# Message stage of a four-layer graph kernel: VectorE copies the turned outer products out of PSUM, and 45 instead of 40 columns of a chunk are summed on TensorE

## The chip, the cores and the metric

The kernel runs on one core of a Trainium2 chip. The metric is the device time in microseconds (us) of one execution. The median of three runs before the change is 27402.7 us. One further execution was profiled; all rows shown here come from it.

## The reference, cut to what matters

Four graph layers are applied in turn to 12500 nodes with 16 features; 400000 edges (`src`, `dst`), sorted by `dst`, are the same in all. Every layer is added to its input. Two of them matter here.

Layer 1 (a sheaf layer) computes two 16-vectors per edge from the features of its two ends and sums one over `src`, one over `dst`. Layer 2 computes a message per edge and sums it over `src`:

```
x_j = h[dst]                                         # 400000 x 16
m   = einsum('ei,ej,ijh->eh', x_j, edge_attr, W)     # outer product 16 x 8 = 128, times W (128 x 16)
m   = silu(m * norm)
agg = segment_sum(m, src)                            # 12500 x 16; W_msg_lin is applied after the sum
u   = silu(einsum('ni,nh,ihk->nk', h, agg, W_upd) * norm2) @ W_upd_lin
x   = x + h + u
```

## The kernel before

**Tiling.** Edges lie on 128 partitions with 3125 columns each (`EP`); a column is one edge per partition. A chunk is `CH` = 125 columns, so both layers run over `NCH` = 25 chunks. All engines have a program of their own over the chunks; the first three chunks are written out, the others are a hardware loop with two chunks in a turn (`chunks`, ring 2). Engines meet at semaphores only, and every engine works strictly in the order of its program.

**The message stage** is `message_edges` (L1711 and on). A chunk is cut into `GR` = 32 groups of 4 columns (the last has 1). For group q:

- VectorE multiplies features and edge attributes to the outer product `PM` (L1909, tile `outer`),
- TensorE transposes it, one 128x128 per column, into PSUM (L1780, `outerT_ps`),
- ScalarE copies that to SBUF (L1848, `outerT`),
- TensorE multiplies by `W_message` (L1790, `message_ps`; `second` in the code),
- ScalarE applies silu and writes `edge_values` (L1830).

`outer`, `outerT_ps` and `outerT` have two buffers each, `message_ps` and `sums_ps` have one.

**Two ways to sum over `src`.** A chunk's first `EQC` = `CH - MT2` = 85 columns are summed within the column first: in groups of `ACCS` = 5, VectorE compares the column's 128 sources with each other (`equal`, L1065, `equal_src`), TensorE multiplies this by the values (`sums`, L1799, `sums_ps`), ScalarE copies the result to `column_sums` (`sums_out`, L1837), and GpSimd adds each column to memory by an indirect DMA (`scatter_pool`, L1199, one DMA a column). The group g is due at step `need[g] + 2`, which gives steps 3 to 23 for the 17 groups.

The other `MT2` = 40 columns are "tiles". For a tile ScalarE makes a one-hot of 1568 node rows in two instructions (L1127 Abs, L1129 Relu; `onehot_act`, a ring of 5 buffers `placed_row`); VectorE splits the values in three bf16 parts and spreads them on 8 lanes (`lane_values`, L1118, per 5 tiles); TensorE adds three parts times four column blocks, 12 matmuls (`tile_sum`, L1141), into PSUM, where the sum stays until the stage ends. The tiles of chunk k are worked off during chunk k+1, spread over its groups by `tiles[q] = range(q * MT2 // GR, (q + 1) * MT2 // GR)`. After chunk 24 its own tiles follow in a tail, then `keep_sums`, `turn_sums` and `store_sums`.

**Order by engine in a step s** (0 to 32) of a chunk:

- TensorE (`products`): `transposes(s)`, `second(s-1)`, the `sums` that are due, then `tile_sum` for `tiles[s-1]` of the chunk before.
- ScalarE (`step`): copy of group s, `silu(s-1)`, the `sums_out` due, then `onehot_act` for `tiles[s]`.
- VectorE (`compute`), ahead of all groups: copy of source and row indices (L1881, L1884; the latter waits until GpSimd has begun the chunk before, `s_chunk`), 16 scans of the features (L1886), then, after the last silu of the chunk before, the split of the tile values (L1890, L1892, L1106, L1108) and the bits of the tile's sources (L1091 to L1096, L1902). Then for each q: `outer` (waits for the transposes of group q-2), the `equal` with `need[g] == q`, the `lane_values` due.
- GpSimd: 85 scatters a chunk, each round of 5 after its `column_sums`.
- SyncE: loads of starts and attributes, and of `src_rows` for `equal`.

**Layer 1** uses the same helpers with its own count of tiles, `MT` = 50, which does not change. It takes `EQC` too: `o.sums = EQC // ACCS` (L1022) is the number of `equal`/`sums` groups at the end of each of its chunks. It scatters 75 columns; groups 15 and 16 (columns 75 to 84) serve only to find, for layer 2, which rows of a column are the first of their source (`CNT`, L1518, L1625 to L1631).

Of the kernel before, what the change touches and what calls it, by code (L numbers as in the profile page):

```python
# [23 lines left out]
ACT = mybir.ActivationFunctionType  # L24
# [3 lines left out]
P = 128  # L28
# [6 lines left out]
CH = 125  # L35
# [4 lines left out]
BIG = 1e30  # L40
HID = 256
ACCS = 5
MT2 = 40
MT = 50
PARTS = 3
Q8 = NP // 8
EQC = CH - MT2
assert EP * P == E and NCH * CH == EP and EQC % ACCS == 0 and MT >= MT2 and (CH - MT) % ACCS == 0


def bcast(ap, shape):
    return ap.to_broadcast(shape)
# [32 lines left out]
def first(k, n):  # L85

    return isinstance(k, int) and k < n


class Kernel:  # L90
# [5 lines left out]
    def sb(self, name, shape, dt=F32, ctx=None):  # L96
        self.uid += 1
        return (ctx or self.ctx).enter_context(self.nc.sbuf_tensor(f"{name}_{self.uid}", shape, dt))
# [5 lines left out]
    def sem(self, name, ctx):  # L104
        self.uid += 1
        s = ctx.enter_context(self.nc.semaphore(f"{name}_{self.uid}"))
        if s.num in self.sem_seen:
            self.sem_old.append(s)
        self.sem_seen.add(s.num)
        return s  # L110
# [1600 lines left out]
    def message_edges(self, Wm, NE_):  # L1711
        nc = self.nc
        W = D + 1
        norm = (D * NE_) ** -0.5
        with ExitStack() as c:
# [5 lines left out]
            PT = [sb(f"outerT{b}", [P, 512]) for b in range(2)]  # L1721
# [5 lines left out]
            o.SRC = srcc  # L1727
            self.tile_buffers(c, o, MT2, [sb(f"placed_row{i}", [P, Q8], BF16)[:] for i in range(5)])
            o.LN = [sb(f"src_row_negative{b}", [P, MT2]) for b in range(2)]
            o.s_abs, o.s_lo = sem("distances_ready"), sem("src_rows_split")  # L1730
            VT, s_vt = sb("matmul_values", [P, MT2, D]), sem("tile_values_ready")
            parts = sb("value_parts", [P, PARTS, MT2, D], BF16)
            keep, turn = sb("node_sums", [P, Q8]), sb("node_rows", [P, -(-Q8 // P) * P])
            tp = [self.ps(f"outerT_ps{i}", [P, 512], c) for i in range(2)]
# [3 lines left out]
            s_used, s_v, s_pm, s_t, s_pt, s_m, s_ms = (sem(x) for x in (  # L1738
                "inputs_used", "dve_chain", "outer_ready", "transposed", "transposed_copied", "message_ready", "message_copied"))
            s_d0 = self.dsem("first_dst_in")  # L1740
            GR, GS = -(-CH // 4), o.sums
# [4 lines left out]
            with self.block() as block:  # L1746
# [74 lines left out]
                @block.scalar  # L1821
                def _(a):
                    def silu(k, q):
                        n = min(4, CH - 4 * q)
                        if q == 0 and not first(k, 1):
                            a.wait_ge(o.s_sum, k * GS)
                        a.wait_ge(s_m, k * GR + (q + 1))
                        if 4 * q + n > SC and not first(k, 1):
                            a.wait_ge(s_vt, k * 2 - 1)
                        nc.scalar.activation(VAL[:, 4 * q:4 * q + n, :], mp[:, 0:n * D].rearrange("p (a b) -> p a b", b=D),  # L1830
                                             ACT.Silu, scale=norm).then_inc(s_ms, 1)

                    def sums_out(k, b, g):
                        if g == 0 and not first(k, 2):
                            a.wait_ge(o.s_chunk, k - 1)
                        a.wait_ge(o.s_sum, k * GS + (g + 1))
                        nc.scalar.activation(o.SV[b][:, ACCS * g:ACCS * (g + 1), :], sm_ps[:, 0:ACCS * D].rearrange("p (a b) -> p a b", b=D),  # L1837
                                             ACT.Copy).then_inc(o.s_sv, 1)

                    def step(k, b):  # L1840
                        for s in range(GR + 1):
                            if s < GR:
                                n = min(4, CH - 4 * s)
                                r = (b + s) % 2
                                a.wait_ge(s_t, k * GR + (s + 1))
                                if not first(k, 1) or s >= 2:
                                    a.wait_ge(s_m, k * GR + (s - 1))
                                nc.scalar.activation(PT[r][:, 0:n * P], tp[r][:, 0:n * P], ACT.Copy).then_inc(s_pt, 1)  # L1848
                            if s >= 1:
                                silu(k, s - 1)  # L1850
                            for g in range(GS):
                                if need[g] + 2 == s:
                                    sums_out(k, b, g)
                            if s < GR and not first(k, 1):
                                if s == 0:
                                    a.wait_ge(o.s_lo, k * 1)
                                for i in tiles[s]:
                                    self.onehot_act(a, o, k - 1, 1 - b, i)
                    chunks(a, NCH, 3, step)
                    a.wait_ge(o.s_lo, NCH)  # L1860
                    for i in range(MT2):
                        self.onehot_act(a, o, NCH - 1, (NCH - 1) % 2, i)

                @block.vector
                def _(v):
# [5 lines left out]
                    def compute(k, b):  # L1871
# [29 lines left out]
                        self.src_bits(v, w, o, srcc[:, SC:CH], b)  # L1901
                        w(v.tensor_scalar(o.LN[b][:], o.LO[b][:], -1.0, None, ALU.mult))  # L1902
                        v.sem_inc(o.s_lo, 1)
                        for q in range(GR):
                            n = min(4, CH - 4 * q)
                            r = (b + q) % 2
                            if not first(k, 1) or q >= 2:
                                v.wait_ge(s_t, k * GR + (q - 1))
                            v.tensor_tensor(PM[r][:, 0:n], bcast(XF[b][:, 4 * q:4 * q + n, :].unsqueeze(3), [P, n, D, NE_]),  # L1909
                                            bcast(EA[b][:, 4 * q:4 * q + n, :].unsqueeze(2), [P, n, D, NE_]), ALU.mult).then_inc(s_pm, 1)  # L1910
                            for g in range(GS):
                                if need[g] == q:
                                    self.equal(v, o, k, b, g)
                            if not first(k, 1):
                                for i in tiles[q]:
                                    if i % ACCS == 0:
                                        self.lane_values(v, o, k - 1, 1 - b, i // ACCS, parts)
                        v.wait_ge(s_pm, k * GR + GR)
                        v.sem_inc(s_used, 1)
                        if first(k, 1):  # L1920
                            K[0] = w.n
                        assert w.n == K[0]
                    chunks(v, NCH, 3, compute)
                    k, b = NCH - 1, (NCH - 1) % 2
                    v.wait_ge(s_ms, NCH * GR)
# [403 lines left out]
```

## Time and profile before

| | us |
|---|---|
| median of 3 runs | 27402.7 |
| range of the 3 runs | 27401.45 to 27413.41 |
| profiled execution, its own time | 27386.06 |
| span of its trace | 27384.3 |
| start of the first and of the last scatter (layer 1; message stage) | 9942.0; 22361.6 |
| message stage, first outer product to release of the next block | 18217.0 to 22368.4 |

Over the whole span GpSimd is busy 73%, TensorE 39%, VectorE 33%, ScalarE 31%. These are averages over stages with different limits; the message stage alone looks quite different, as its window below shows. In the profile, PE is TensorE's matmul, PEld its weight load (each matmul of these small shapes has one, and consecutive loads show the pace of TensorE), DVE VectorE, ACT ScalarE, POOL GpSimd. A timeline row is: start, duration, engine, line, operation, tiles, count, and in brackets the idle time ahead of it and what ended it. ScalarE and VectorE start an instruction a little before the one ahead has ended, so the pace is read from start to start.

### The profile page before, as it was taken

What the parts mean: (1) busy time and instruction counts of PE and PEld (TensorE: products, weight loads), DVE (VectorE), ACT (ScalarE), POOL (GpSimd) and SP (SyncE); (2) the same over time, 40 slices, a digit from 0 to 9 for tenths busy, and PEclk for the clock granted to TensorE, in tenths of its full rate; (3) what the DMA queues carried; (4) which work ended last, traced back from release to release, by engine and by line L of the source; (5) the groups of instructions that cost most, each with busy time, mean ns of one, the idle gap of its engine ahead of it and who ended that gap; (6) DMA issues with size and microseconds to landing.
All of it is one profiled execution on the core that took longest, in us unless ns stands there. A gap on an engine that the chain in (4) does not pass through costs nothing. (4 is left out here: it accounts for less than half of the span.)

```text
span 27384.3 us, 206288 instructions
## 1 busy us (share of the span) xinstructions
PE 10673.4 (39%) x61414; PEld 7318.9 (27%) x61414; DVE 9052.7 (33%) x15004; ACT 8400.1 (31%) x8986; POOL 20052.3 (73%) x17824
## 2 busy tenths in 40 slices
PE   0000000100000057777776676749998874000004
PEld 0000000100000034444444444436666653000003
DVE  2333333222222133333333333324433322333331
ACT  0000000000000035555555555638888860000001
POOL 5777776677777577777777777568888863777775
PEclk9999999555555568888888778869999987555557
DMA  2111111111111112222222222123333324666664
GB/s 79 30 30 36 30 30 31 18 27 27 27 30 27 22 29 29 29 29 29 29 29 29 32 36 30 22 49 49 51 50 50 49 24 131 204 207 203 203 207 123
DMA packets 2038400, 1639.07 MB, mean 60 GB/s; under 512 B 868362, under 2 KB 1838548, under 8 KB 2020260
## 3 DMA queue, kind: packets, MB, share of 16 engines
q0 software_dynamic: 1061008, 588.28, 15.9%
q10 hardware_dynamic: 818050, 577.62, 6.4%
q1 hardware_dynamic: 158354, 460.98, 4.9%
q8 instruction: 499, 8.18, 0.1%
q14 instruction: 489, 4.01, 0.0%
HBM read 938.69 MB, written 686.90 MB: 59 GB/s over the span
## 5 line engine op out<-in xcount | busy, mean ns | idle before, releaser
L1199 POOL DMA_INDIRECT acc<-column_sums,sum_rows x4000 | 6639.9, 1660 | 1441.3 <-issue 1179.9
L717 POOL DMA_INDIRECT gathered<-gat_table,src_index x6250 | 6052.3, 968 | 2053.5 <-issue 2053.5
L1141 PE MATMUL node_sums<-placed_row,lane_values 128*128 128x392 bf16 x27000 | 5155.9, 345 | 1193.0 <-ACT placed_row L1129 1079.8
L1419 POOL DMA_INDIRECT gathered<-sheaf_table,src_index x3125 | 3156.4, 1010 | 1233.5 <-issue 875.7
L2137 POOL DMA_INDIRECT gathered<-message_table,src_index x3125 | 3062.1, 980 | 984.7 <-issue 951.7
L1127 ACT ACTIVATE placed_row<-iota_rows,src_row_negative 128x1568 bf16<-128x1568 f32 x2250 | 3582.3, 1592 | 269.7 <-PE node_sums L1141 205.4
L1141 PEld LDWEIGHTS node_sums<-placed_row,lane_values 128*128 128x128 bf16 x27000 | 2620.1, 103 | 3477.1 <-ACT placed_row L1129 1558.0
L1129 ACT ACTIVATE placed_row<-placed_row 128x1568 bf16<-128x1568 bf16 x2250 | 3397.5, 1510 | 71.1
L829 PE MATMUL histogram<-high_onehot,low_onehot 128*128 128x98 bf16 x3125 | 368.4, 279 | 7793.2 <-DVE high_onehot L743 7793.2
L816 ACT ACTIVATE decays<-decays 128x375 f32<-128x375 f32 (+1 forms) x50 | 20.6, 412 | 8226.1 <-DVE weights L787 8226.1
L829 PEld LDWEIGHTS histogram<-high_onehot,low_onehot 128*128 128x128 bf16 x3125 | 235.1, 131 | 7926.3 <-DVE high_onehot L743 7926.3
L777 DVE TENSOR_TENSOR scores<-alpha_dst,gathered 128x375 f32<-128x375 f32 (+1 forms) x50 | 34.8, 696 | 5633.9 <-DMA gathered<-gat_table,src_index 5633.9
L567 PE MATMUL transposed<-ident,last_rows 128*128 128x128 f32 (+3 forms) x5 | 2.2, 442 | 4223.6 <-DVE sums L599 4223.6
L2154 DVE SCALAR_TENSOR_TENSOR gathered<-gathered,same 128x256 f32<-128x256 f32 x3000 | 1472.1, 491 | 107.2
L1475 PE MATMUL hidden_row_ps<-vectors,equal_src 128*128 128x19 f32 x4250 | 911.3, 380 | 1157.8 <-DVE equal_src L1065 1065.2
L2270 ACT ACTIVATE sumsT<-ps 128x512 f32<-128x512 f32 x49 | 29.3, 597 | 4084.0 <-PE ps L2238 4084.0
L1909 DVE TENSOR_TENSOR outer<-dst_features,edge_attr 128x512 f32<-128x512 f32 (+1 forms) x800 | 543.4, 679 | 2175.3 <-PE outerT_ps L1780 2169.8
L1475 PEld LDWEIGHTS hidden_row_ps<-vectors,equal_src 128*128 128x128 f32 x4250 | 908.5, 333 | 1178.4 <-DVE equal_src L1065 1037.2
L1118 DVE TENSOR_TENSOR lane_values<-lane_onehot,products 128x640 bf16<-128x640 bf16 x750 | 572.2, 821 | 1898.0 <-PE node_sums L1141 1892.0
L567 PEld LDWEIGHTS transposed<-ident,last_rows 128*128 128x128 f32 (+3 forms) x5 | 0.7, 149 | 4225.2 <-DVE sums L599 4225.2
L1579 DVE COPY vectors<-vectors_ps 128x512 f32<-128x512 f32 x200 | 138.4, 692 | 2628.1 <-PE vectors_ps L1458 2628.1
L1455 PEld LDWEIGHTS vectors_ps<-W_blocks,hidden 128*128 128x128 f32 x6400 | 822.9, 194 | 364.8 <-issue 199.1
(397 smaller groups left out, 17322.3 us busy)
## 6 DMA issues: line engine op xcount, KB each, us to landing
message_rows<-gathered ACTq DMA_DIRECT2D x250, 1600.0 KB
src_rows<-src_rows SPq DMA_DIRECT2D x225, 640.0 KB
src_rows<-src_rows SPq DMA_DIRECT2D x125, 960.0 KB
gathered<-gat_table,src_index POOLq DMA_INDIRECT x6250
gat_rows<-scanned ACTq DMA_DIRECT2D x25, 3375.0 KB
acc<-column_sums,sum_rows POOLq DMA_INDIRECT x4000, 3.1
gat_rows<-scanned ACTq DMA_DIRECT2D x25, 2125.0 KB, 6.8
start_values<-starts SPq DMA_DIRECT2D x50, 1062.5 KB, 5.0
```

The costliest lines, as they stand in the source:

```text
L717: g.indirect_dma_start(G[b][:, j, :], None, tab, bass.IndirectOffsetOnAxis(ap=IX[b][:, j:j + 1], axis=0)).then_inc(s_g[b], 16)
L829: last = pe.matmul(hp[:, 0:NT], OL[ob][:, j, :], OH[ob][:, j, :], start=opening and j == 0, stop=False, skip_group_check=True)
L1118: ins = v.tensor_tensor(o.SVH[r][:, i], bcast(o.E8[:, a:a + ACCS, :].unsqueeze(3), [P, ACCS, 8, D]), bcast(parts[:, i, a:a + ACCS, :].unsq ...
L1127: self.nc.scalar.activation(o.OW[r], o.IO[:], ACT.Abs, bias=o.LN[b][:, i:i + 1]).then_inc(o.s_abs, 1)
L1129: self.nc.scalar.activation(o.OW[r], o.OW[r], ACT.Relu, scale=-1.0, bias=1.0).then_inc(o.s_mv, 1)
L1141: last = pe.matmul(o.acc[:, m, 0:Q8 // 4], lane, o.OW[r][:, m * (Q8 // 4):(m + 1) * (Q8 // 4)], start=first(k, 1) and i == 0 and part == 0 ...
L1199: g.indirect_dma_start(self.acc[i], bass.IndirectOffsetOnAxis(ap=o.IXS[b][:, j:j + 1], axis=0), o.SV[b][:, j, :], None, compute_op=ALU.add ...
L1419: g.indirect_dma_start(G[b][:, j, :], None, self.tab17, bass.IndirectOffsetOnAxis(ap=IX[b][:, j:j + 1], axis=0)).then_inc(s_g[b], 16)
L1455: last = pe.matmul(vp[:, (4 * i + j) * 32:(4 * i + j + 1) * 32], R[j % 2][:, i * P:(i + 1) * P], W2b[:], start=i == 0 and j == 0, stop=Fal ...
L1475: last = pe.matmul(pre[g % 2][:, j * DW:(j + 1) * DW], o.EQ[g % o.nq][:, j, :], VAL[:, g * ACCS + j, :], start=True, stop=True)
L2137: g.indirect_dma_start(G[b][:, j, :], None, self.qtab, bass.IndirectOffsetOnAxis(ap=IX[b][:, j:j + 1], axis=0)).then_inc(s_g[b], 16)
L2154: v.scalar_tensor_tensor(G[b][:, j, :], before, SM[b][:, j:j + 1], G[b][:, j, :], ALU.mult, ALU.add).then_inc(s_v, 1)
```

## The change

Two things. ScalarE's program loses the copy of `outerT_ps`; VectorE's gets it as `turned(q)`, with the same two waits (for the transposes of q, and for the product that read the buffer two groups ago). In VectorE's order `turned(q - 1)` stands behind `outer` of group q and ahead of `equal` and `lane_values` of q; `turned(31)` stands behind the loop, ahead of the next chunk's work. And `MT2` is 45, so that `EQC` is 80: 16 groups of sums (due at steps 3 to 21) and 80 scatters a chunk in the message stage, 45 tiles, 9 `lane_values`; and 16 groups in each chunk of layer 1.

```diff
-MT2 = 40
+MT2 = 45
@@ ScalarE, step
                         for s in range(GR + 1):
-                            if s < GR:
-                                n = min(4, CH - 4 * s)
-                                r = (b + s) % 2
-                                a.wait_ge(s_t, k * GR + (s + 1))
-                                if not first(k, 1) or s >= 2:
-                                    a.wait_ge(s_m, k * GR + (s - 1))
-                                nc.scalar.activation(PT[r][:, 0:n * P], tp[r][:, 0:n * P], ACT.Copy).then_inc(s_pt, 1)
                             if s >= 1:
                                 silu(k, s - 1)
@@ VectorE, compute
                         v.sem_inc(o.s_lo, 1)
+                        def turned(q):
+                            n = min(4, CH - 4 * q)
+                            r = (b + q) % 2
+                            v.wait_ge(s_t, k * GR + (q + 1))
+                            if not first(k, 1) or q >= 2:
+                                v.wait_ge(s_m, k * GR + (q - 1))
+                            v.tensor_copy(PT[r][:, 0:n * P], tp[r][:, 0:n * P]).then_inc(s_pt, 1)
                         for q in range(GR):
...
                                             bcast(EA[b][:, 4 * q:4 * q + n, :].unsqueeze(2), [P, n, D, NE_]), ALU.mult).then_inc(s_pm, 1)
+                            if q:
+                                turned(q - 1)
                             for g in range(GS):
...
+                        turned(GR - 1)
                         v.wait_ge(s_pm, k * GR + GR)
                         v.sem_inc(s_used, 1)
```

## Rows read from the trace of the kernel before

**Rows 1.** Windows, message stage: us; busy PE, PEld, DVE, ACT, POOL; clock, DMA, GB/s.

```profile
18640.00:20880.00 2240.00, 2038.49 (x14374) 1526.52 (x14372) 889.73 (x1466) 2003.80 (x2259) 1889.42 (x1151) 0.96 0.34 51
```

**Rows 2.** Groups by line in 19000 to 21000: busy, mean ns, idle before and releasers.

```profile
L1199 POOL DMA_INDIRECT acc<-column_sums,sum_rows x1027 | 1687.6, 1643 | 313.1 <-issue 298.1 <-DMA acc<-column_sums,sum_rows 11.6 <-ACT column_sums L1837 3.4
```

**Rows 3.** Timeline of DVE: last outer products of chunks 1, 16, 24; two copies.

```profile
18477.22 0.29 DVE L1909 TENSOR_TENSOR outer<-dst_features,edge_attr 128x128 f32<-128x128 f32 x1 [5.97 <-PE outerT_ps L1780]
...
20874.20 0.29 DVE L1909 TENSOR_TENSOR outer<-dst_features,edge_attr 128x128 f32<-128x128 f32 x1 [5.97 <-PE outerT_ps L1780]
20877.73 0.23 DVE L1881 COPY src_chunk<-srcf 128x125 f32 x1 [3.24 <-issue]
...
22041.29 0.23 DVE L1884 COPY sum_rows<-sidx 128x125 int32 x1 [14.00 <-POOLq L1198]
...
22191.67 0.29 DVE L1909 TENSOR_TENSOR outer<-dst_features,edge_attr 128x128 f32<-128x128 f32 x1 [5.97 <-PE outerT_ps L1780]
```

**Rows 4.** Timeline of one step with sums and one tile, ACT and PEld.

```profile
20004.34 1.59 ACT L1127 ACTIVATE placed_row<-iota_rows,src_row_negative 128x1568 bf16<-128x1568 f32 x1
...
20005.84 0.53 PEld L1780 LDWEIGHTS outerT_ps<-ident,outer 128*128 128x128 f32 x4
...
20007.22 1.20 PEld L1799 LDWEIGHTS sums_ps<-edge_values,equal_src 128*128 128x128 f32 x10
...
20007.38 0.58 ACT L1848 ACTIVATE outerT<-outerT_ps 128x512 f32<-128x512 f32 x1
20007.86 0.21 ACT L1830 ACTIVATE edge_values<-message_ps 128x64 f32<-128x64 f32 x1
...
20008.26 1.86 PEld L1141 LDWEIGHTS node_sums<-placed_row,lane_values 128*128 128x128 bf16 x12
...
20008.56 0.24 ACT L1837 ACTIVATE column_sums<-sums_ps 128x80 f32<-128x80 f32 x1 [0.48 <-PE sums_ps L1799]
...
20010.19 0.52 PEld L1780 LDWEIGHTS outerT_ps<-ident,outer 128*128 128x128 f32 x4
```

**Rows 5.** Timeline: second tile of a step, from its Relu to its matmuls.

```profile
20017.71 1.51 ACT L1129 ACTIVATE placed_row<-placed_row 128x1568 bf16<-128x1568 bf16 x1
...
20019.27 1.77 PEld L1141 LDWEIGHTS node_sums<-placed_row,lane_values 128*128 128x128 bf16 x12 [0.44 <-ACT placed_row L1129]
```

**Rows 6.** Timeline from one chunk to the next, and the next chunk's last silu.

```profile
20077.28 0.29 DVE L1909 TENSOR_TENSOR outer<-dst_features,edge_attr 128x128 f32<-128x128 f32 x1 [5.97 <-PE outerT_ps L1780]
...
20085.39 0.26 ACT L1848 ACTIVATE outerT<-outerT_ps 128x128 f32<-128x128 f32 x1
...
20091.94 0.49 DVE L1890 COPY matmul_values<-edge_values 128x640 f32<-128x640 f32 x1 [7.48 <-ACT edge_values L1830]
...
20098.38 0.69 DVE L1909 TENSOR_TENSOR outer<-dst_features,edge_attr 128x512 f32<-128x512 f32 x1 [0.23 <-DVE src_row_negative L1902]
...
20104.67 0.22 ACT L1830 ACTIVATE edge_values<-message_ps 128x64 f32<-128x64 f32 x1
...
20250.38 0.17 ACT L1830 ACTIVATE edge_values<-message_ps 128x16 f32<-128x16 f32 x1
```

**Rows 7.** Windows: the ten microseconds after a chunk change.

```profile
20100.00:20110.00 10.00, 8.38 (x45) 5.99 (x44) 7.01 (x11) 8.83 (x10) 8.47 (x6) 0.65 0.49 103
```

**Rows 8.** Groups of the page: a copy of this size on DVE.

```profile
L1579 DVE COPY vectors<-vectors_ps 128x512 f32<-128x512 f32 x200 | 138.4, 692 | 2628.1 <-PE vectors_ps L1458 2628.1
```

**Rows 9.** Timeline of the stage's end: second store of tile sums, last scatter, next block.

```profile
22335.70 0.75 SPq L1177 DMA_DIRECT2D acc_matmul<-node_rows  x1
...
22361.64 1.55 POOL L1199 DMA_INDIRECT acc<-column_sums,sum_rows  x1 [0.30 <-issue]
22368.40 11.99 SPq L1220 DMA_DIRECT2D acc_in<-acc  x5
```

**Rows 10.** Timeline of layer 1's groups of sums, one of them.

```profile
12191.94 0.83 DVE L1065 TENSOR_TENSOR equal_src<-src_rows,src_chunk 128x640 f32<-128x640 f32 x1 [1.31 <-PE hidden_row_ps L1475]
```

**Rows 11.** Waits of POOL in 12000 to 14000: us, times, longest.

```profile
POOL gathered L1419 <- DVEq L1632: 70.7, 6, 14.3
```

## The prediction

> **What bounds the kernel now.** The page's shares are averages over stages, so the message stage is read by itself, in five views.
>
> First its window [rows 1]: in 2240 us PE is busy 2038, ACT 2004, POOL 1889, DVE 890. Three engines are nearly full; which of them ends last can't be told from shares. Second, the groups by line [rows 2]: POOL issued 1027 scatters in 2000 us, 1.95 us each, and its idle time is almost all "issue", the gap between two of its own instructions; it waited for ACT 3.4 us in all. So POOL never starves: 85 scatters take 165.5 us. Third, the chunk's length, read at the last outer product [rows 3]: from chunk 1 to 16 it is (20874.20 - 18477.22) / 15 = 159.8 us, from chunk 16 to 24 (22191.67 - 20874.20) / 8 = 164.7 us. TensorE, ScalarE and VectorE (the lattice, below) make a chunk in 159.8, POOL falls 5.7 behind in each, and once it is a chunk behind, VectorE waits for it ahead of its row indices (14.00 us at 22041.29). Fourth, the end [rows 9]: the next block starts 6.8 us after the last scatter; the tile sums were stored some 26 us sooner. So POOL sets the stage, but the lattice is only 5.7 us a chunk shorter.
>
> Fifth, the timeline of one step [rows 4], which gives prices from start to start. TensorE: transposes and products of a group 1.38 (05.84 to 07.22), a group of sums 1.04 (to 08.26), a tile 1.93 (to 10.19). ScalarE: a one-hot 3.04 (04.34 to 07.38), the copy 0.48 (to 07.86), silu and column sums about 0.11 each when not waiting (between 0 and their busy 0.21 and 0.24). In this step both need 4.35: TensorE because 1.38 + 1.04 + 1.93 is that, ScalarE with 0.48 of waiting for the sums. Before the change a chunk has 12 such steps, 11 with one tile and no sums (3.04 + 0.48 + 0.11 = 3.63, ScalarE last) and 8 with two tiles (6.67, ScalarE last): 52.2 + 39.9 + 53.4 = 145.5. The trace has 20250.38 - 20104.67 = 145.7 from the first silu to the last [rows 6]. The prices can be trusted.
>
> **The change, part by part.**
>
> *POOL.* 5 scatters fewer a chunk: 80 x 1.947 = 155.8. Alone this takes the stage down to the lattice's pace, since that now ends last; so all depends on what the lattice becomes.
>
> *ScalarE.* Loses 31.25 x 0.48 = 15.0 and one column sum, gains 5 x 3.04 = 15.2: its work stays as it was, 142 us.
>
> *TensorE.* 5 tiles more, one group of sums less: 5 x 1.93 - 1.04 = +8.6 us a chunk. This is no longer covered: steps 3 to 21 hold 27 tiles and 16 sums, 19 x 1.38 + 16 x 1.04 + 27 x 1.93 = 94.9 us for TensorE against 27 x 3.04 + 19 x 0.11 + 16 x 0.11 = 86 for ScalarE. TensorE ends last in all of them. ScalarE can't run ahead through it: its silu of step s follows TensorE's product in the same step, so a step with two tiles hands over late. From Relu to the matmuls it takes 1.56 [rows 5]; worked through for the 8 steps with two tiles in that stretch (2, 4, 7, 9, 12, 14, 17, 19), the second tile comes 0.2 to 0.3 late each time, 2.3 in all. So 97.2. Ahead of it stand 6.0 from the first silu to step 3 (unchanged). Behind it, steps 22 to 31 have no sums and 15 tiles: ScalarE last, 15 x 3.04 + 9 x 0.11, 1.7 to start, and five times 0.1 to 0.5 in which TensorE is late after a pair, 1.7 together: 50.0. First to last silu: 6.0 + 97.2 + 50.0 = 153.2. The same walk over the old order gives 145.1, so the step costs 8.1. The bounds: if hand-overs are free, TensorE's and ScalarE's stretches give 149.2, +4; if every step costs the later engine's price (2.42 + 3.86 for the two-tile steps with sums, 6.2 for those without), +10.
>
> *Chunk change.* From the last silu VectorE splits the tile values and prepares the bits, 20091.94 to 20098.38, then outer, transposes, copy, product, silu, 20104.67 [rows 6]. Five of the ops in it work on 40 columns and now on 45: a tenth of about 5 us, +0.6; the copy moves to VectorE at 0.69 us (a copy of this size there [rows 8]) against 0.58 and stands behind lane_values and a second outer, +0.1. Between +0.3 and +1.5; I take +0.7.
>
> *The copy on VectorE within a chunk.* 31 x 0.69 + 0.29 = 22 us a chunk beside 64 busy of 160: hidden by idle time. What stands behind each is equal (0.82) and lane_values (2.3); outer of group q+1 is then done at most 5 us after the transposes of q-1, and TensorE wants it 6.6 after. PT is ready 1.6 after the transposes, and its product comes at least 3.3 after. Nothing, if that holds; if not, up to 1 us in each of 9 groups.
>
> *The copy at the end of a chunk.* turned(31) now stands ahead of the next chunk's scans. In [rows 6] VectorE was done with outer 31 at 77.57, and with the scans 7.48 before it was let go by the last silu, at 84.5. It will start them only after the copy of group 31 (ACT made it at 85.39; VectorE can at about 84.2), that is 7 us later. So the cover shrinks from 7.48 to about 0. In each second chunk, at the end of the hardware loop's turn, VectorE has another 3.24 us of issue [rows 3]: this stood in the cover and now is bare, 3.2 / 2 = +1.6 a chunk. Bounds 0 and 3.2.
>
> Together 8.1 + 0.7 + 1.6 = +10.4: a chunk of 170.2, TensorE and ScalarE last, POOL (155.8) well inside. Even if every added copy stretched one scatter from 1.55 to 1.80, POOL would need 164.
>
> *The stage.* 23 chunk distances x 10.4 + 8.8 for the first (its change is short) = +248. The pushback goes: 8 x (164.7 - 159.8) = -39. The first chunk, without tiles, loses one group of sums, -2. The tail: TensorE's and ScalarE's end now decides, not POOL's. Its store was issued at 22335.70; with the same 6.8 to the next block that is 22342.5, plus 5 tiles x 3.04 = 15.2, plus 2.0 because the last silu lies further behind the last outer: 22359.7 against 22368.4, -9. Sum +198.
>
> *Layer 1.* One group of 17 less. The groups pass at 0.83 + 1.31 = 2.14 us [rows 10], VectorE, TensorE and ScalarE in turn, and VectorE goes on from the last to the next chunk. POOL has 70.7 / 6 = 11.8 us of slack a chunk there, waiting for VectorE [rows 11], so it doesn't hold this back. 25 x 2.14 = -54. Bounds 0 and -60 (narrower index work besides).
>
> Net +198 - 54 = +144 on the profiled execution's 27386.1, which lies 16.6 under the median; the same on the median 27402.7 gives 27547, I say 27545.
>
> Of TensorE's clock [rows 7]: after a chunk change 0.65 of full is granted in ten us, so part of it at 1.2 GHz; before, TensorE had sat idle some 5 us. It will idle as long, and 3 us longer in each second chunk. The Trainium skill (TensorE: Matmul & The Clock Gate, Part 1) says that the clock follows how busy the array has been of late. By that rule the slow stretch grows in those chunks; the row agrees that it exists, and can't show the growth.
>
> The Trainium skill (VectorE: DVE Perf Modes, the errata's table) prices a PSUM source at 120 + elements cycles on VectorE and 172 + elements on ScalarE's faster clock: 0.66 against 0.57 us here. The trace agrees (0.69 and 0.58); the rule speaks against the move, and by it the copies cost VectorE 20 us a chunk, still hidden.
>
> **The rivals.**
>
> *TensorE hides the tiles (the faster side).* It is idle 9% of the window [rows 1], 14 us a chunk, more than the added 8.6. If this idle time is usable in the sums' stretch, a chunk stays at 159.8 and the stage loses the pushback: 27402.7 - 39 - 2 - 9 - 54 = 27299. Against it: half of the idle time lies at the chunk change and the rest in steps where ScalarE is last, not in steps 3 to 21. It decides only if a step with sums goes on at 4.35 while it holds 1.42 tiles on average, which is 5.16 by price. If POOL were last even so, at 155.8, it would be 27299 - 24 x 4.0 = 27203.
>
> *Only TensorE's price is paid.* Hand-overs cost nothing, and VectorE's back edge is covered: +4.7 to 6.5 a chunk. With 6: 24 x 6 - 39 - 11 - 54 = +40, 27443. For it: five buffers for one-hots. Against it: ScalarE's order ties it to TensorE's step, and the late second tile is there in [rows 5].
>
> *Dearer chunk change.* Scans bare in every chunk (the copy of 31 waits, +3.2 instead of 1.6), slow clock for one more step (+2): +3.6 x 24 = 86 more, 27630. With layer 1's gain lost as well it would be 27685.
>
> **How the numbers follow.** Forecast 58%, at 27545, its own range 27480 to 27600. TensorE hides 8%, POOL last 2%: faster. Only TensorE's price 17%, of which two thirds within 0.2% (0.2%, 55 us, is about what a measurement of this kernel tells from no change: 27348 to 27458). Dearer change 15%. So faster 0.10, same 0.13, slower 0.77. The range for 8 in 10 is 27430 to 27625: it leaves out the faster side and the far end of the dearer one.
>
> **What would show it.** The last outer products 170 us apart, without idle time at POOL's index wait. PEld without gaps in the steps with sums, and ACT waiting there for message_ps and sums_ps. POOL waiting for column_sums, 14 us a chunk. DVE's wait for the last silu near 0 in place of 7.48. The next block released by the store of tile sums. In layer 1, chunks 2.1 us shorter. It would be wrong if chunks were at 160 or less, if ScalarE had no waits in the sums' stretch, or if VectorE's outer came late in mid-chunk.

## The result and the profile after

| | before | after |
|---|---|---|
| median, us | 27401.4 | 27506.0 |
| range of 6 runs each | 27397.48 to 27413.41 | 27483.06 to 27519.65 |
| span of the profiled execution | 27384.3 | 27484.5 |

The ratio is 1.0037 (95% interval 1.0026 to 1.0047): 104.6 us slower, where +144 was forecast. In the traces the next block is released 107.4 us later, and this divides so: the message stage starts 54.3 sooner (first outer product at 18162.70 in place of 18217.0), the way from there to the last outer product of chunk 0 is 1.4 shorter, the 24 distances from that one to the last outer product of chunk 24 add up to 4041.8 in place of 3866.8 (+175.0), and the tail is 11.9 shorter. -54.3 - 1.4 + 175.0 - 11.9 = +107.4. What follows the release is 7.2 shorter, which gives the +100.2 of the spans. The stage alone, from its first outer product to the release, is 4313.1 in place of 4151.4, +161.7.

The 54.3 are themselves two things. These are the last gather of layer 0 and layer 1's first group of sums, before and then after:

```profile
9132.99 0.95 POOL L717 DMA_INDIRECT gathered<-gat_table,src_index  x1 [0.30 <-issue]
...
9887.90 1.56 DVE L1065 TENSOR_TENSOR equal_src<-src_rows,src_chunk 128x640 f32<-128x640 f32 x2
```

```profile
9146.31 0.94 POOL L717 DMA_INDIRECT gathered<-gat_table,src_index  x1 [0.30 <-issue]
...
9900.59 1.56 DVE L1065 TENSOR_TENSOR equal_src<-src_rows,src_chunk 128x640 f32<-128x640 f32 x2
```

From that group to the first outer product of the message stage it takes 8262.1 in place of 8329.1, so layer 1 is 66.9 shorter. But it starts 12.7 later, and that lateness is there at the end of layer 0 already (13.3), in which the change alters nothing. The same point lay up to 20 us apart in the traces of e5 to e8 (10675.0 to 10695.5), which have the same layer 0 too, so it is scatter between executions.

The first view is the window of the stage, columns as in [rows 1]:

```profile
18600.00:20960.00 2360.00, 2148.80 (x15042) 1578.84 (x15041) 1180.12 (x1946) 2007.24 (x1932) 1841.04 (x1128) 0.97 0.31 46
```

VectorE's share went from 40% to 50%, TensorE's stayed at 91%, ScalarE's fell from 89 to 85% and GpSimd's from 84 to 78%. Who lost its cover stands in the groups by line and in the waits (line waited for: us in total, times, longest), both of 19000 to 21000:

```profile
L1199 POOL DMA_INDIRECT acc<-column_sums,sum_rows x949 | 1548.8, 1632 | 440.3 <-issue 267.1 <-ACT column_sums L1837 157.4 <-DMA acc<-column_sums,sum_rows 15.8
```

```profile
DVE outerT L1903 <- PE outerT_ps L1780: 955.8, 315, 5.5
ACT edge_values L1830 <- PE message_ps L1790: 194.3, 154, 12.4
POOL acc L1199 <- ACT column_sums L1837: 157.4, 21, 16.7
PE outerT_ps L1780 <- DVE outer L1909: 106.6, 24, 9.4
ACT column_sums L1837 <- PE sums_ps L1799: 83.0, 94, 0.9
DVE matmul_values L1883 <- ACT edge_values L1830: 2.0, 6, 0.3
```

GpSimd, which waited for ScalarE 3.4 us in [rows 2], now waits 157.4, that is 13 us a chunk: it no longer sets the pace, and its scatters aren't slower for VectorE's added copies (1632 ns against 1643). ScalarE waits for TensorE's products. TensorE waits for an outer product 24 times in 12 chunks, which is twice at each chunk change and never within a chunk, and the waits show none for one of VectorE's copies. Of VectorE's wait for the last silu (7.48 in [rows 6]) at most 0.3 is left.

The pace, from VectorE's timeline as in [rows 3] (last outer products of chunks 1, 11, 12 and 24):

```profile
18430.47 0.28 DVE L1909 TENSOR_TENSOR outer<-dst_features,edge_attr 128x128 f32<-128x128 f32 x1
...
20116.36 0.28 DVE L1909 TENSOR_TENSOR outer<-dst_features,edge_attr 128x128 f32<-128x128 f32 x1
...
20283.48 0.28 DVE L1909 TENSOR_TENSOR outer<-dst_features,edge_attr 128x128 f32<-128x128 f32 x1
...
22310.96 0.28 DVE L1909 TENSOR_TENSOR outer<-dst_features,edge_attr 128x128 f32<-128x128 f32 x1
```

The mean distance is (22310.96 - 18430.47) / 23 = 168.7; from chunk 4 on 167.1 and about 170.8 take turns, 169.0 on average, and there is no later stretch with a slower pace, as there was with 164.7 before.

One step with sums and two tiles, loads of TensorE and ScalarE's instructions, to be laid beside [rows 4, 5]:

```profile
20046.33 0.53 PEld L1780 LDWEIGHTS outerT_ps<-ident,outer 128*128 128x128 f32 x4
...
20047.71 1.20 PEld L1799 LDWEIGHTS sums_ps<-edge_values,equal_src 128*128 128x128 f32 x10
...
20048.74 1.86 PEld L1141 LDWEIGHTS node_sums<-placed_row,lane_values 128*128 128x128 bf16 x12
20049.48 1.51 ACT L1129 ACTIVATE placed_row<-placed_row 128x1568 bf16<-128x1568 bf16 x1
20050.90 0.21 ACT L1830 ACTIVATE edge_values<-message_ps 128x64 f32<-128x64 f32 x1
20051.00 0.23 ACT L1837 ACTIVATE column_sums<-sums_ps 128x80 f32<-128x80 f32 x1
20051.04 1.77 PEld L1141 LDWEIGHTS node_sums<-placed_row,lane_values 128*128 128x128 bf16 x12 [0.43 <-ACT placed_row L1129]
...
20052.88 0.53 PEld L1780 LDWEIGHTS outerT_ps<-ident,outer 128*128 128x128 f32 x4
```

The prices are those of before: 1.38 to the sums, 1.03 to the first tile. The second tile is late for its Relu. The step takes 6.55 where the prices give 1.38 + 1.04 + 3.86 = 6.28: 0.27 late, within the 0.2 to 0.3 that was forecast.

Two chunk changes, one within the loop's turn and one at its end:

```profile
20125.20 0.29 DVE L1903 COPY outerT<-outerT_ps 128x128 f32<-128x128 f32 x1 [5.52 <-PE outerT_ps L1780]
20125.55 0.23 DVE L1874 COPY src_chunk<-srcf 128x125 f32 x1
...
20132.20 0.17 ACT L1830 ACTIVATE edge_values<-message_ps 128x16 f32<-128x16 f32 x1
...
20132.40 0.54 DVE L1883 COPY matmul_values<-edge_values 128x720 f32<-128x720 f32 x1 [0.33 <-ACT edge_values L1830]
...
20145.39 0.22 ACT L1830 ACTIVATE edge_values<-message_ps 128x64 f32<-128x64 f32 x1 [9.99 <-PE message_ps L1790]
...
20292.32 0.29 DVE L1903 COPY outerT<-outerT_ps 128x128 f32<-128x128 f32 x1 [5.53 <-PE outerT_ps L1780]
20295.69 0.23 DVE L1874 COPY src_chunk<-srcf 128x125 f32 x1 [3.07 <-issue]
...
20299.32 0.17 ACT L1830 ACTIVATE edge_values<-message_ps 128x16 f32<-128x16 f32 x1
...
20302.42 0.54 DVE L1883 COPY matmul_values<-edge_values 128x720 f32<-128x720 f32 x1
...
20315.85 0.22 ACT L1830 ACTIVATE edge_values<-message_ps 128x64 f32<-128x64 f32 x1 [11.84 <-PE message_ps L1790]
```

The first to the last silu, 20145.39 to 20299.32, takes 153.9. The change takes 13.2 in the first case. In the second, after 3.07 of issue, the scans end after the silu that VectorE used to wait for, and the change takes 16.5. The clock granted around the first silu of a chunk (a window that lies to it as that of [rows 7] does, from 4.67 us ahead of it) is 0.57, lower than the 0.65 of [rows 7]:

```profile
20140.72:20150.72 10.00, 8.38 (x40) 5.90 (x39) 6.69 (x11) 3.30 (x4) 4.70 (x3) 0.57 0.14 4
```

The end of the stage, against [rows 9]:

```profile
22339.09 1.55 POOL L1199 DMA_INDIRECT acc<-column_sums,sum_rows  x1 [0.30 <-issue]
...
22470.98 0.66 SPq L1177 DMA_DIRECT2D acc_matmul<-node_rows  x1
22475.80 11.74 SPq L1220 DMA_DIRECT2D acc_in<-acc  x5
```

The last scatter is over 135 us before the next block starts. That starts 4.8 after the store of the tile sums.

### The profile page after: what moved, and what is told of

Same layout as the page of the kernel before. It is cut to its first block and busy times, and to the rows that moved or that the text cites. A ratio compares the mean times of both kernels' runs of the same rounds, so it can differ in the third digit from the quotient of the medians.

```text
span 27484.5 us, 208040 instructions
## 1 busy us (share of the span) xinstructions
PE 10857.1 (40%) x62414; PEld 7393.0 (27%) x62414; DVE 9540.5 (35%) x15829; ACT 8407.1 (31%) x8386; POOL 19794.9 (72%) x17699
## 5 line engine op out<-in xcount | busy, mean ns | idle before, releaser
L1199 POOL DMA_INDIRECT acc<-column_sums,sum_rows x3875 | 6419.4, 1657 | 1684.0 <-issue 1130.8
L1141 PE MATMUL node_sums<-placed_row,lane_values 128*128 128x392 bf16 x28500 | 5421.0, 344 | 1159.9 <-ACT placed_row L1129 1038.9
L1127 ACT ACTIVATE placed_row<-iota_rows,src_row_negative 128x1568 bf16<-128x1568 f32 x2375 | 3777.9, 1591 | 277.0 <-PE node_sums L1141 198.6
L1141 PEld LDWEIGHTS node_sums<-placed_row,lane_values 128*128 128x128 bf16 x28500 | 2772.8, 103 | 3552.7 <-ACT placed_row L1129 1525.3
L1129 ACT ACTIVATE placed_row<-placed_row 128x1568 bf16<-128x1568 bf16 x2375 | 3586.3, 1510 | 75.1
L816 ACT ACTIVATE decays<-decays 128x375 f32<-128x375 f32 (+1 forms) x50 | 20.6, 412 | 8219.1 <-DVE weights L787 8219.1
L2157 DVE SCALAR_TENSOR_TENSOR gathered<-gathered,same 128x256 f32<-128x256 f32 x3000 | 1469.7, 490 | 107.4
L1903 DVE COPY outerT<-outerT_ps 128x512 f32<-128x512 f32 (+1 forms) x800 | 541.9, 677 | 2017.9 <-PE outerT_ps L1780 1998.6
```

Source lines behind the costliest of these rows:

```text
L1127: self.nc.scalar.activation(o.OW[r], o.IO[:], ACT.Abs, bias=o.LN[b][:, i:i + 1]).then_inc(o.s_abs, 1)
L1129: self.nc.scalar.activation(o.OW[r], o.OW[r], ACT.Relu, scale=-1.0, bias=1.0).then_inc(o.s_mv, 1)
L1141: last = pe.matmul(o.acc[:, m, 0:Q8 // 4], lane, o.OW[r][:, m * (Q8 // 4):(m + 1) * (Q8 // 4)], start=first(k, 1) and i == 0 and part == 0 ...
L1199: g.indirect_dma_start(self.acc[i], bass.IndirectOffsetOnAxis(ap=o.IXS[b][:, j:j + 1], axis=0), o.SV[b][:, j, :], None, compute_op=ALU.add ...
L2157: v.scalar_tensor_tensor(G[b][:, j, :], before, SM[b][:, j:j + 1], G[b][:, j, :], ALU.mult, ALU.add).then_inc(s_v, 1)
```

## The experiments

The experiments ran on three chips (e1 to e4, e5 to e8, and e9 and e10), and there everything but the message stage took longer than in the first runs, for the kernel before as for all others: its medians are 29697.5, 29379.8 and 29351.7 in place of 27401.4. In the traces the message stage begins some 1500 to 2000 us later and what follows it is some 380 longer. So totals are compared only with those of before beside them. The message stage is nearly the same everywhere (4313.1, and 4314.9 for the changed kernel run again), and its length, from first outer product to release, is compared directly.

| run | stage, us | chunks, us | ratio of totals (95%) |
|---|---|---|---|
| before | 4151.4 | 159.8, then 164.7 | |
| after | 4313.1 | 167.1 / 170.8 | 1.0037 (1.0026 to 1.0047) |
| e1, copy moved, 40 tiles | 4130.8 | 157.0 / 160.1, then 164 | 0.9995 (0.9982 to 1.0007) |
| e2, 45 tiles, copy on ScalarE | 4359.1 | 170.7 | 1.0053 (1.0038 to 1.0069) |
| e3, layer 1 with 17 groups | 4315.5 | 167.2 / 170.8 | 1.0049 (1.0035 to 1.0064) |
| e4, last copy on ScalarE | 4279.5 | 167.1 / 167.4 | 1.0024 (1.0014 to 1.0034) |
| e5, one-hots three tiles ahead | 4147.4 | 160.5 / 163.7 | 0.9978 (0.9966 to 0.999) |
| e6, e4 and e5 together | 4083.1 | 159.1 | 0.9954 (0.9942 to 0.9967) |
| e7, the changed kernel again | 4314.9 | 167.2 / 170.7 | 1.0037 (1.0025 to 1.0049) |
| e8, e3 again, beside e7 | 4314.8 | as e7 | 1.0068 (1.0055 to 1.0081) |
| e9, e6 with a later split | 4238.7 | 164.5 / 166.6 | 1.001 (0.9997 to 1.0023) |
| e10, e6 again, beside e9 | 4072.9 | 157.7 / 159.7 | 0.9957 (0.9941 to 0.9973) |

**e1_copy_only: the copy is moved, the tiles stay at 40.**

```diff
-MT2 = 45
+MT2 = 40
```

> VectorE copies the turned products, MT2 stays 40. My theory (the slowdown is TensorE's five more tiles in the steps with sums, less what ScalarE is relieved of): a chunk of the lattice needs about 6 + 98 + 34 from first to last silu and 15 for the chunk change, 153 us; POOL's 85 scatters take 165.5 and stay last from the first chunk on. So the time is that of the kernel before, 27402, within 15 us, and the pushback of VectorE by POOL is there from early chunks on. Rival (the copy on VectorE is what costs: late outer products, bare scans, slower scatters beside more VectorE work): 30 to 100 us slower than before, with scatters above 1.66 us on average or POOL waiting for column sums.

TensorE, ScalarE and VectorE now make a chunk in 157.0 and 160.1 by turns, 158.2 on average and so 1.6 less than before, but GpSimd's 85 scatters stay, and from chunk 15 on the chunks are 164 apart. In 21000 to 23000 GpSimd waits for ScalarE 4 us in all, and from 22700 to 24100 VectorE waits for GpSimd ahead of its row indices:

```profile
L1199 POOL DMA_INDIRECT acc<-column_sums,sum_rows x1031 | 1685.9, 1635 | 314.2 <-issue 301.1 <-DMA acc<-column_sums,sum_rows 9.1 <-ACT column_sums L1837 4.0
```

```profile
DVE sum_rows L1877 <- POOLq L1198: 24.3, 4, 7.6
```

The stage is 20.6 shorter, the total no different that can be measured. The moved copy by itself costs nothing. The time was as expected, the way there was not: the 153 us expected for a chunk without GpSimd were 5 too low, and the pushback came no earlier than in the kernel before.

**e2_tiles_only: 45 tiles, the copy stays on ScalarE** (against the kernel before).

```diff
-MT2 = 40
+MT2 = 45
```

> MT2 = 45, ScalarE keeps the copy. My theory: ScalarE is last in 31 steps, 13 x 6.7 + 12 x 4.27 + 6 x 3.63 = 160 us from first to last silu, 13.2 + 1.3 for the chunk change (scans hidden as before): a chunk of 174.6 against 169.0 of the changed kernel, so 24 x 5.6 = 134 us slower than it, about 27640 (+0.86% on the kernel before). Rival (the copy on VectorE is what costs): faster than the changed kernel, 27400 to 27460, because layer 1's 54 us are gained and nothing is lost.

All of the loss is in the tiles: 170.7 a chunk in place of 159.8, the stage +207.7. The 174.6 that was expected was too high by 4, and the total came out 0.53% above before where 0.86% was expected. First to last silu takes 157.1 where 160 was worked out. ScalarE's timeline shows why:

```profile
21196.24 0.58 ACT L1848 ACTIVATE outerT<-outerT_ps 128x512 f32<-128x512 f32 x1
21196.72 0.22 ACT L1830 ACTIVATE edge_values<-message_ps 128x64 f32<-128x64 f32 x1
21196.82 0.24 ACT L1837 ACTIVATE column_sums<-sums_ps 128x80 f32<-128x80 f32 x1
21196.94 1.61 ACT L1127 ACTIVATE placed_row<-iota_rows,src_row_negative 128x1568 bf16<-128x1568 f32 x1
...
21200.00 0.58 ACT L1848 ACTIVATE outerT<-outerT_ps 128x512 f32<-128x512 f32 x1
```

In the step after a pair (a step with two tiles) ScalarE is the one behind: it finds the product and the sums ready and needs 3.76, not TensorE's 4.35. So lateness doesn't add up: it changes hands after each pair. The copy's move, at 45 tiles, takes the stage from 4359.1 to 4313.1, so 46 us, more than twice what it gives at 40 tiles, where GpSimd holds the pace.

**e3_layer1_17_groups: the changed kernel, but layer 1 keeps 17 groups.**

```diff
+EQ1 = 85
...
-            o = self.scatter_buffers(c, SC, 2, 2)
+            o = self.scatter_buffers(c, SC, 2, 2, EQ1)
```

Layer 1's slices for `CNT`, `FST`, `IXF`, `IXS` and `VAL` are taken with `EQ1` as well.

> The changed kernel, but layer 1 keeps its 17 groups of sums a chunk (85 columns), message stage as changed. My theory: layer 1's gain of 2.14 us a chunk is undone, +54 us on the changed kernel, 27560. Rival (layer 1 hides it, and the message stage alone costs 104): no difference from 27506.

The stage is that of the changed kernel (4315.5), as it should be. The changed kernel itself did not run beside it, so the gain of the missing group can't be read from it; e7 and e8 below mend that.

**e4_last_copy_act: the changed kernel, but ScalarE copies group 31**, ahead of silu 30; `turned(31)` goes.

```diff
                         for s in range(GR + 1):
+                            if s == GR - 1:
+                                n, r = CH - 4 * s, (b + s) % 2
...
+                                nc.scalar.activation(PT[r][:, 0:n * P], tp[r][:, 0:n * P], ACT.Copy).then_inc(s_pt, 1)
                             if s >= 1:
                                 silu(k, s - 1)
@@ VectorE
-                        turned(GR - 1)
```

> The changed kernel, but the copy of a chunk's last group (one column) is made by ScalarE ahead of its silu of group 30, so that VectorE begins the next chunk's scans after turned(30). My theory: chunks of the changed kernel alternate 167.1 and 170.8 because of the loop's back edge laid bare on VectorE; with the cover back both are 167.1 to 167.4, 12 x 3.7 = 44 us less, about 27465. Rival (the alternation is TensorE's clock after the longer idle time): unchanged, 27500, and 170 still alternates.

This is the cleanest of the answers. The long chunks are gone (167.1 / 167.4), the stage is 33.6 shorter. That is less than the 44 expected, which took 12 long chunks of 3.7: the trace of the changed kernel has 10, each 3.4 longer than e4's. The back edge is still there, but covered again:

```profile
21816.10 0.25 DVE L1880 COPY src_chunk<-srcf 128x125 f32 x1 [2.99 <-issue]
...
21825.87 0.54 DVE L1889 COPY matmul_values<-edge_values 128x720 f32<-128x720 f32 x1 [3.15 <-ACT edge_values L1830]
```

After 2.99 of issue VectorE has 3.15 to spare ahead of the last silu. So one small copy, of a single column, uncovered some 3.4 us in every second chunk.

**e5_ahead3: the changed kernel, but ScalarE makes three one-hots more at step 0 and stays three ahead.**

```diff
-                                for i in tiles[s]:
+                                ahead = 3
+                                lo = 0 if s == 0 else min(MT2, tiles[s - 1].stop + ahead)
+                                for i in range(lo, min(MT2, tiles[s].stop + ahead)):
```

> The changed kernel, but ScalarE makes the one-hots three tiles ahead (step 0 makes tiles 0 to 3, each later step the tiles three further on; the ring of five allows it), so that its idle time after the last silu is used. My theory (in the changed kernel TensorE is last in the steps with sums, ScalarE in the ten behind them, and both idle at the chunk change): the late hand-overs go (2.3) and the steps 22 to 31 fall to TensorE's price (50 to about 39 up to the last silu); the last silu then comes before VectorE's scans are done, which lie bare by 4 or 7 us. A chunk of 159.0 and 162.2 in turn, 160.6 on average against 169.0: 24 x 8.4 = 200 us less in the message stage than the changed kernel's. Rival (TensorE alone sets the changed kernel's chunk, by 45 tiles): chunks stay above 166.

**e6_ahead3_last_act: the same with e4's copy on ScalarE.**

> As e5, and the last group's copy on ScalarE as in e4. My theory: the scans start 5 us sooner, a chunk of 155.2 and 158.1 in turn, 156.7 on average, which is POOL's own 155.8: both last. 24 x 12.3 = 295 us less in the message stage than the changed kernel's, some 130 less than in the kernel before; with layer 1's gain about 190 us faster than the kernel before (27215 where that takes 27400). Rival (the copy on VectorE is what bounds the stage in the end, by late outer products): chunks of 160 or more, no faster than e5.

Five buffers hold one-hots, and the order of ScalarE's program used one or two of them. With three ahead, the stage is 167.5 (e5) and 231.8 (e6) shorter than the changed kernel's beside them (e7), and e6 beats both kernels in the total too. So the ring could have hidden nearly all that the tiles cost, and the second rival's argument (five buffers for one-hots) held once ScalarE's order let it. Both fell short of what was expected, though, by 1.5 (e5) and 2.4 us (e6) a chunk: in steps with sums TensorE's loads have no gap, and TensorE's own work is the bound. In the window of 21000 to 23320, e6:

```profile
21000.00:23320.00 2320.00, 2198.86 (x15650) 1649.11 (x15649) 1232.70 (x2024) 2090.37 (x2027) 1902.81 (x1170) 0.97 0.34 49
```

PE is busy 95%, and GpSimd waits for ScalarE still, 61 us in 2000. What the order alone would give the kernel with 40 tiles was not run.

**e7_changed_again and e8_layer1_17_again: the changed kernel and e3 on one chip.**

> The changed kernel again, beside the others on one chip. My theory: chunks of 167.1 and 170.8 as before on any chip; its total 104 us above the kernel before where layer 1 runs as in the first profile, with a message stage 162 us longer and a layer 1 54 us shorter.

> The changed kernel with 17 groups in layer 1, beside the changed kernel on one chip (e3 had no changed kernel beside it). My theory: 54 us slower than the changed kernel, within the scatter of that chip's layer 1; message stage the same. Rival: no difference.

The 17th group costs 29563.55 - 29490.79 = 73 us where 54 was forecast, and the runs don't overlap (29415 to 29523 against 29538 to 29618). Layer 1's chunks are uneven on this chip (some 340 to 380 us all but the last, where they were 319 to 328 in the first two traces), so the 73 is a rough figure. The changed kernel's ratio is again 1.0037, though the whole takes 7% longer here.

**e9_late_split and e10_ahead3_again: e6 with the split of the tile values ahead of outer product 2, and e6 once more.**

```diff
-            tiles = [range(q * MT2 // GR, (q + 1) * MT2 // GR) for q in range(GR)]
+            tiles = [range(max(q - 2, 0) * MT2 // (GR - 2), max(q - 1, 0) * MT2 // (GR - 2)) for q in range(GR)]
@@ VectorE, compute
                         for q in range(GR):
+                            if q == 2:
+                                tile_values()
...
-                                v.wait_ge(s_t, k * GR + (q - 1))
+                                v.wait_ge(s_t, k * GR + (q - 1 if q else 0))
```

> The kernel with the one-hots three tiles ahead and the last group's copy on ScalarE, and besides VectorE splits the tile values and prepares the tile bits of a chunk only ahead of its outer product 2, not ahead of outer product 0; the 45 tiles of a chunk are spread over steps 2 to 31 in place of 0 to 31. If the stretch between the last silu of a chunk and the first of the next (13 us) is what is left above POOL's price, because TensorE stands behind the split there: it now does the transposes and products of groups 0 and 1 beside the split, POOL's 80 scatters (155.8 us) end last, chunks are 156 to 157 us apart in place of 159.1, and the message stage is 23 x 2.6 = 60 us shorter (about 4025 us), some 0.2% of the whole. Rival: what is left is TensorE's own work (loads without gaps in the steps with sums, now with 45 tiles in 30 steps in place of 32); the split only stands later, chunks stay at 158 to 160 and the time is that of the kernel without this edit within 0.1%.

> The kernel with the one-hots three tiles ahead and the last group's copy on ScalarE once more, beside the one with the late split: the ratio to the kernel before is again about 0.995, chunks 159.1 us apart and a message stage of about 4087 us. If the earlier gain was that of one chip, the ratio lies above 0.998.

The idea of e9 fell, and its rival too: the chunks are 164.5 and 166.6 apart, 7 more than e10's. Its chunk change:

```profile
21830.63 1.29 DVE L1920 TENSOR_TENSOR outer<-dst_features,edge_attr 128x512 f32<-128x512 f32 x2
...
21835.04 0.97 PEld L1790 LDWEIGHTS message_ps<-W_message,outerT 128*128 128x128 f32 x8 [0.67 <-DVE outerT L1912]
...
21835.69 0.61 DVE L1892 COPY matmul_values<-edge_values 128x720 f32<-128x720 f32 x1
...
21842.99 0.69 DVE L1920 TENSOR_TENSOR outer<-dst_features,edge_attr 128x512 f32<-128x512 f32 x1 [0.15 <-DVE src_row_negative L1904]
...
21843.73 0.71 PEld L1780 LDWEIGHTS outerT_ps<-ident,outer 128*128 128x128 f32 x4 [7.72 <-DVE outer L1920]
```

TensorE got the transposes of two groups and the products of one done first, in 2.5 us, and then stood for 7.72, longer than the 5.5 that is e10's longest such wait. It had no more to do: the products of group 1 stand behind the transposes of group 2 in its program, these wait for the outer product behind the split, and without the split there are no tiles either. From the last silu to silu 4 of the next chunk it takes 34.0 and 36.2 by turns, e10 35.3 and 37.3: the move gave 1.2 us. But at that point 3 tiles are summed in place of 5, which is 3.9 us of TensorE's work still to do, and the rest of the chunk takes 130.4 in place of 122.5. Half of these 8 us is the two tiles; of the other half more than 2 are ScalarE's waits for a one-hot buffer (39.9 us in 21000 to 23000, 10.0 in e10), with more pairs in the steps with sums. The rest of it wasn't taken apart. e10 repeats e6 (0.9957 against 0.9954): the gain is not that of one chip.

## Why the prediction was right

Forecast was +144, measured +104.6, by the mechanism that was forecast: five more tiles that TensorE and ScalarE can't cover, and a back edge laid bare. Some of its sizes were off, and one that fitted did so by luck. By its steps:

- *GpSimd at 155.8 well inside: right.* It waits 13 us a chunk (14 forecast), and nothing of the stretch with 164.7 is left. The last scatter is long over when the tile sums are stored.
- *Tiles are no longer covered, +8.1: right, but +7.0 on average.* First to last silu 153.2 forecast, 153.9 measured, with 1.38, 1.04 and 1.93 as read from [rows 4]. But the stretch of before from which the difference was taken, 145.7 in [rows 6], is the shortest of four kinds. In eight chunks in a row of before it is 145.7, 146.6, 147.0 and 147.3 by turns, since the first step after the change takes 4.4, 5.3, 5.7 or 6.0; over chunks 1 to 15 the mean is 146.9. In the changed kernel this step takes 4.9 to 5.5. The working explained 145.5 of a chunk, and its walk gave 145.1.
- *Chunk change +0.7: too high, +0.3.* 13.2 against 12.9.
- *Back edge +1.6: right.* The change takes 16.4 to 17.1 in place of 13.2 in every second chunk, and e4 takes that away. That is +1.8 a chunk from chunk 4 on, and +1.6 over the 23 distances, since 10 of them have a back edge.
- Together +8.9, and +8.9 by the mean distances too (168.7 - 159.8), where 10.4 was forecast. Over 24 distances, with the pushback gone, +175 in place of 23 x 10.4 + 8.8 - 39 = +209. **This term, a chunk 1.5 too long, is 34 of the 39 us by which the forecast was high.** 1.1 of the 1.5 come from checking the walk against a single sampled chunk, 0.4 from the chunk change; no mechanism was missing.
- *First chunk -2, tail -9:* -1.4 and -11.9. 2.0 of the 2.9 at the tail are the way from the store to the next block, 4.8 where 6.8 was taken over from the last scatter.
- *Layer 1 -54: met by luck.* The stage does start 54.3 sooner, but layer 1 itself gave 66.9, more than the 60 that was its bound, 2.7 a chunk where 2.14 was read from one group in [rows 10], and the 12.7 by which layer 0 ended later in this execution hid the difference. e7 and e8 give 73.
- *The copy within a chunk is free: right.* No outer product came late in mid-chunk, and e1 shows no loss by it. The rule on PSUM sources in the Trainium skill (VectorE: DVE Perf Modes, the errata's table) spoke against the move, and was near the price of one copy (0.66 by the rule, 0.69 measured), which stayed hidden.
- *The rivals.* "TensorE hides the tiles" failed for this order of the program: the sums' stretch was gapless at its prices. "Only TensorE's price is paid" failed too: the second tile of a step is late and the back edge is bare. e5 shows that most of this was ScalarE's order all the same, since it takes back 6.9 of the 9.2 us that a chunk is longer from chunk 4 on: late hand-overs were not forced by the hardware, but by the place of the one-hots. "Dearer chunk change" didn't come: the scans were bare in every second chunk only, and the slow clock after the change was no dearer than before on average: the first step takes 5.2 where the mean of before is 5.4 to 5.5.

The four kinds go with the clock. In windows that all begin 4.67 us ahead of a chunk's first silu it is 0.65 in [rows 7], in the chunk of 4.4, then 0.56, 0.52 and, in the chunk of 6.0, 0.50, which is all at 1.2 GHz; the changed kernel has 0.55 to 0.58 in every chunk looked at, with first steps of 5.1 to 5.5. The last of these windows, of the kernel before:

```profile
20578.11:20588.11 10.00, 8.38 (x35) 6.04 (x34) 5.91 (x9) 7.90 (x8) 8.48 (x6) 0.50 0.47 103
```

[Rows 7] thus showed the best of four, and the prediction took it for all. The Trainium skill (TensorE: Matmul & The Clock Gate, Part 1) lets the clock follow how busy the array was; the rows agree that a slow stretch follows each stop. That it would grow with a longer stop was the prediction's own step, and the rows don't bear it out: TensorE stands 5.4 us at a change without a back edge and 6.7 to 7.6 at one with it, and the clock is 0.56 to 0.57 and 0.55 to 0.58, the first step 5.2 to 5.4 and 5.1 to 5.5.

What is open: why the clock of before takes turns over four chunks, and why one group of sums less shortens a chunk of layer 1 by 2.7 us where its row gives 2.14 (the narrower index work that the prediction named may be part of it; no run parts the two).

## What to carry to other kernels

When two engines are within a few per cent of the bound, taking work off the one that ends last pays only as much as the next one leaves: price a step for every engine from its own row, add the steps up in order, and let lateness change hands. Average such a sum over several chunks before taking a difference. And when an engine loses work, look whether its order can now run further ahead, since that was worth more here (168 us) than the change itself cost (162); and look at the last instruction ahead of a loop's back edge: what it waits for decides whether the back edge is covered.

## What the runs showed of the hardware

- VectorE has 3.0 to 3.8 us of "issue" ahead of the first instruction after the loop's back edge, once in each of its 10 turns, in the kernel before as in the changed one. It costs nothing as long as a longer wait stands behind it (e4 had 3.15 us of it left), and about all of it when that wait is gone (the chunk change takes 3.2 to 3.9 more).
- After 5.4 us without work TensorE's loads ran at half pace: 12 loads of a tile took 3.8 us (20144.98 to 20148.74) in place of 1.93, at a granted clock of 0.50 in that stretch, which is 1.2 GHz. Moving the split in e9 moved this stop and made it longer (7.72), not shorter.
- The same kernel took 7 to 8% longer in the experiments than in the first runs, and the message stage no more than 0.04% longer. A gather in layer 0 took 1050 ns in place of 967 (mean of 6250), while the indirect scatters of the message stage took 1634 ns in both. Whether this is the chip or something else that differed wasn't tested. Between e6 and e10, the same kernel on two chips, the stage differs by 10 us, or 0.25%, all of it in the first steps of the chunks (the rest of a chunk, from silu 4 on, takes 122.5 in both). So a stage's own length is the better measure across chips, to about that.
